# Depthwise convolutions of a focal-modulation block: diagonal products and vector taps replaced by products with banded matrices

## The reference, cut to what matters

```python
y = einsum('bhwc,cd->bhwd', layernorm(x), Wf) + bf
q, ctx, gates = y[..., :32], y[..., 32:64], y[..., 64:68]
ctx_all = 0
for l, k in enumerate((k0, k1, k2)):          # depthwise, 3x3, 5x5, 7x7, 'SAME'
    ctx = gelu(dwconv_same(ctx, k))
    ctx_all = ctx_all + ctx * gates[..., l:l + 1]
ctx_global = gelu(mean(ctx, axis=(1, 2)))
ctx_all = ctx_all + ctx_global * gates[..., 3:]
x_out = q * (einsum('bhwc,cd->bhwd', ctx_all, Wh) + bh)
x = x + (einsum('bhwc,cd->bhwd', layernorm(x_out) * gamma + beta, Wp) + bp)
# then a recurrent layer, a two-directional state-space layer, a mixture of experts
```

## Time and profile before

| | |
|---|---|
| median of 3 runs | 858.18 us (853.11, 858.18, 858.95) |
| the profiled execution | 853.12 us, span 851.2 us |
| PE | 680.4 us busy, 80% of the span, 8288 MATMUL |
| PEld | 416.7 us busy, 49% |
| DVE | 701.4 us busy, 82% |
| ACT | 362.5 us busy, 43% |
| POOL | 478.3 us busy, 56% |
| mean granted clock of TensorE | 0.943 |

### The profile page before, as it was taken

One profiled execution on the slowest core, in us unless ns is written; L12 is line 12 of the kernel. 1 busy time (PEld: TensorE's weight loads), 2 busy tenths in 40 slices (PEclk: granted clock), 3 DMA queues, 4 the chain that ended last, 5 costly groups with the idle time before them and its releaser, 6 DMA issues. The chain is left out here.

```text
span 851.2 us, 19699 instructions
## 1 busy us (share of the span) xinstructions
PE 680.4 (80%) x8288; PEld 416.7 (49%) x8288; DVE 701.4 (82%) x917; ACT 362.5 (43%) x577; POOL 478.3 (56%) x243
## 2 busy tenths in 40 slices
PE   7887786779977658887888788888878887787496
PEld 3554453346645325555555555555554554454142
DVE  3998889664334089999999999999999999995785
ACT  2230001146642755655565555555655665431000
POOL 5000000000001089999999999999999999990000
PEclk9999998789979959999999999999999999998697
DMA  4000000000000737887778777877897787740001
GB/s 177 5 4 4 4 5 4 2 1 1 1 2 16 181 100 187 204 225 205 198 207 229 196 208 202 224 207 201 204 225 202 201 227 206 197 113 2 1 12 47
DMA packets 35080, 102.95 MB, mean 121 GB/s; under 512 B 6768, under 2 KB 8944, under 8 KB 34992
## 3 DMA queue, kind: packets, MB, share of 16 engines
q1 hardware_dynamic: 34768, 100.84, 45.3%
q0 software_dynamic: 224, 0.85, 0.2%
HBM read 98.13 MB, written 3.54 MB: 119 GB/s over the span
## 5 line engine op out<-in xcount | busy, mean ns | idle before, releaser
L547 POOL TENSOR_TENSOR ring<-ring,big 128x1152 f32<-128x1152 f32 x74 | 193.7, 2630 | 4.0 <-DVE ring L923 4.0
L189 PE MATMUL banks<-ring,main_params 128*128 128x288 f32 x592 | 174.0, 423 | 0.6 <-POOL ring L547 0.6
L701 ACT ACTIVATE big<-big,small 128x576 f32<-128x576 f32 x192 | 142.5, 765 | 30.3 <-DVE ring L923 15.8
L923 DVE TENSOR_TENSOR_SCAN ring<-big,banks 128x576 f32<-128x576 f32 x111 | 146.1, 1339 | 1.5
L911 DVE TENSOR_TENSOR banks<-banks,big 128x576 f32<-128x576 f32 x192 | 141.3, 743 | 2.9 <-POOL big L533 1.6
L523 POOL COPY big<-normed 128x288 f32<-128x288 f32 x8 | 3.0, 430 | 242.2 <-DVE normed L443 242.2
L1234 PE MATMUL banks<-big,selectors 96*128 96x512 bf16 x192 | 72.8, 390 | 70.2 <-DVE ring L923 39.9
L189 PEld LDWEIGHTS banks<-ring,main_params 128*128 128x128 f32 x592 | 105.3, 191 | 36.1 <-issue 4.0
L377 PE MATMUL banks<-big 32*32 32x288 f32 x3712 | 96.7, 429 | 21.5 <-issue 17.5
L547 POOL TENSOR_TENSOR normed<-normed,big 128x1152 f32<-128x1152 f32 x36 | 94.4, 2631 | 0.9 <-DVE normed L923 0.9
L781 DVE SCALAR_TENSOR_TENSOR big<-big 128x288 f32<-128x288 f32 x216 | 93.6, 510 | 0.0
(11 more groups left out here) (179 smaller groups left out, 1016.3 us busy)
## 6 DMA issues: line engine op xcount, KB each, us to landing
big<-bc_rows SPq DMA_DIRECT2D x256, 288.0 KB, 4.3
big<-bc_rows SPq DMA_DIRECT2D x128, 144.0 KB, 4.4
bc_rows<-big SPq DMA_DIRECT2D x16, 144.0 KB, 3.3
residual<-x_in SPq DMA_DIRECT2D x2, 576.0 KB, 6.0
out<-big SPq DMA_DIRECT2D x16, 72.0 KB, 1.8
experts<-experts_in SPq DMA_DIRECT2D x1, 896.0 KB, 9.4
main_params<-main_in SPq DMA_DIRECT2D x1, 639.0 KB, 8.2
big<-front_in POOLq DMA_DIRECT2D x1, 574.5 KB, 5.9
```

The source lines that it names most:

```text
L189: last = nc.tensor.matmul(PS[rows, 2 * p + a, 0:HALF], lhsT, rhs[:, bass.ds(at + a * HALF, HALF)], start=start, stop=stop, skip_group_chec ...
L547: nc.gpsimd.tensor_tensor(slots, slots, CT[k % 5], ALU.mult).then_inc(weighted, 1)
L701: nc.scalar.activation(out, DT[b % 3], ACT.Exp, scale=ANEG[:, s:s + 1]).then_inc(decay_set, 1)
L923: nc.vector.tensor_tensor_scan(slot, DECAY[m % 3], place, 0.0, ALU.mult, ALU.add).then_inc(scanned, 1)
```

## The change

The first layer is laid out anew. The context goes through the convolutions with image columns on the partitions: partition 32 j + x holds column x of the images j of all four groups, and the free axis is channel, group, row (`CT0`, `A1`, `B2`, `C3`). A convolution of one channel along a row is then a product with a 32 x 32 banded matrix, and the rows' offsets dy are taken by shifted reads. For every level, every block k of four channels, every offset dy, every strip r and every channel q of the block there is one 32 x 32 matmul with 4 (24 - |dy|) columns, at most 96. No tap is left on VectorE.

The new pieces: the banded matrices are computed on the host and loaded (11,520 columns of fp32 on 128 partitions, 5.9 MB, three transfers on SP between x and the rest of `main_params`). ctx and the gates are produced row by row, with the image row as the stationary operand and 36 columns of Wf as the moving one. VectorE copies them out in three instructions, multiplies every level with its gate (`gate`), and turns the products back to channels on partitions (`turn`, 32 x 32 transposes). Sums for the global context are 48 matmuls with 64 columns.

```diff
-            for cp in CP:
-                nc.gpsimd.memset(cp, 0.0).then_inc(pads_zero, 1)
...
+            for l in range(LEVELS):
+                part = slice(TW_AT[l], (TW_AT + [TW_W])[l + 1])
+                sp.dma_start(TW[:, part], toeplitz_in[:, part]).then_inc(toeplitz_loaded[l], 16)
...
+            def ctx_rows(ys):
+                for y in ys:
+                    a, at = y // (H // 2), y % (H // 2) * (C + 4)
+                    for g in range(GROUPS):
+                        rows = slice(C * g, C * (g + 1))
+                        for j in range(J):
+                            last = nc.tensor.matmul(PS[C * j:C * (j + 1), 4 * a + g, at:at + C + 4],
+                                                    XNW[rows, j * L + y * W:j * L + y * W + 32], fpar("wcg")[rows, :],
+                                                    start=True, stop=True)
...
+            def conv_block(l, kh, k):
+                src = by_channel((CT0[:, 0:TB], A1, B2)[l])
+                for i, dy in enumerate(offsets(l)):
+                    ys = slice(max(0, -dy), H - max(0, dy))
+                    there = slice(ys.start + dy, ys.stop + dy)
+                    for r in range(GROUPS):
+                        rows = slice(C * r, C * (r + 1))
+                        for q in range(GROUPS):
...
+                            last = nc.tensor.matmul(dst.rearrange("p (g y) -> p g y", g=GROUPS)[:, :, ys], TW[rows, at:at + 32],
+                                                    src[rows, k, q, :, there], start=i == 0, stop=i == KS[l] - 1)
...
+            for l in range(LEVELS):
+                pe.wait_ge(toeplitz_loaded[l], 16)
+                for kh in range(2):
+                    if l == 0:
+                        pe.wait_ge(ctx_dve, 2 + kh)
...
+                        pe.wait_ge(gelu_set, 2 * (l - 1) + kh + 1)
...
+                    for k in range(4 * kh, 4 * kh + 4):
+                        last = conv_block(l, kh, k)
...
+                    last.then_inc(tap_mm, 1)
+            for kh in range(2):
+                pe.wait_ge(gelu_set, 2 * 2 + kh + 1)
...
+                for y in range(H):
+                    last = nc.tensor.matmul(PS[:, 4 * kh, 0:64], fpar("sumx"), per_row[:, :, y], start=y == 0, stop=y == H - 1)
+                last.then_inc(sum_mm, 1)
...
+            for a in range(2):
+                dve.wait_ge(mod_mm, a + 1)
+                for j in range(J):
...
+                    nc.vector.scalar_tensor_tensor(out=GLOBAL[:, here], in0=GLOBAL[:, here], scalar=GADD[:, j:j + 1],
+                                                   in1=PS[:, 4 * a + j, 0:HALF], op0=ALU.mult, op1=ALU.add).then_inc(glob_added, 1)
```

More of the change, by code:

```diff
@@ L248, in build_program @@
[L248 to L259, removed]
@@ L507, in _ @@
             pool.dma_start(RSEL, rows_in).then_inc(rows_loaded, 16)
-            for cp in CP:
-                nc.gpsimd.memset(cp, 0.0).then_inc(pads_zero, 1)
[L511 to L517, removed]
+            nc.gpsimd.memset(XNW[:, N:N + 8], 0.0).then_inc(tail_zero, 1)
             for a in range(2):
@@ L593, in _ @@
+            act.wait_ge(gadd_mm, 1)
+            nc.scalar.activation(GADD, PS[:, 5, 0:J], ACT.Copy).then_inc(gadd_set, 1)
             ln_act(act, 1, 1)
@@ L1054, in _ @@
             pe.wait_ge(front_loaded, 16)
-            pe.wait_ge(main_loaded, 16)
-            for a in range(2):
-                pe.wait_ge(ln_out, a + 1)
-                strips(quad_bank(a), own(fpar("wctx")), plain(XN, a), True, True).then_inc(ctx_mm, 1)
+            pe.wait_ge(tail_zero, 1)
+            def ctx_rows(ys):
[7 more added lines that the diff above has]
+                                                    start=True, stop=True)
+                return last
@@ new lines, in _, with spread_gates @@
+            pe.wait_ge(ln_out, 1)
+            ctx_rows(range(H // 2 - 1))
+            pe.wait_ge(ln_out, 2)
+            ctx_rows([H // 2 - 1]).then_inc(ctx_mm, 1)
+            ctx_rows(range(H // 2, H)).then_inc(ctx_mm, 1)
+            def spread_gates():
+                gates = CT0[:, TB:TB + 4 * ROWS].rearrange("p (l c) -> p l c", l=4)[:, 0:3:2, :]
+                pe.wait_ge(ctx_dve, 3)
+                for j in range(J):
+                    rows = slice(C * j, C * (j + 1))
+                    last = nc.tensor.matmul(PS[:, 4 + j, 0:2 * ROWS], fpar("rep")[rows, :], gates[rows], start=True, stop=True)
+                last.then_inc(rep_mm, 1)
@@ L1107, in _ @@
-            pe.wait_ge(gelu_set, 4 + 2 * GROUPS)
-            pe.wait_ge(gated, 6 * GROUPS)
-            for a in range(2):
-                strips(quad_bank(a), own(fpar("wh")), plain(ALLT, a), True, False)
-            for j in range(J):
-                pe.wait_ge(glob_added, j + 1)
-                for a in range(2):
-                    last = nc.tensor.matmul(PS[:, 4 * a + j, 0:HALF], fpar("wh"),
-                                            ALLC[:, j * L + a * HALF:j * L + (a + 1) * HALF], start=False, stop=True)
@@ new lines, in modulate @@
+            def modulate(a):
+                pe.wait_ge(turned_p, 2 * 1 + a + 1)
+                strips(quad_bank(a), own(fpar("wh")), lambda rows, c: turned_row(P1T, a)[rows, c, :, 0:W], True, False)
+                by_j(a, P0T, False)
+            pe.wait_ge(glob_set, 1)
+            modulate(0)
+            pe.wait_ge(turned_p, 2 * 2 + 1)
+            by_j(0, P2T, True).then_inc(mod_mm, 1)
+            pe.wait_ge(glob_mask, 1)
+            for g in range(GROUPS):
+                last = nc.tensor.matmul(PS[C * g:C * (g + 1), 5, 0:J], fpar("whu"), GMASK[:, g * J:(g + 1) * J],
+                                        start=True, stop=True)
```

335 lines of the change are left out of this document (165 added, 170 removed).

## The result

The changed kernel took 893.5 us (median of 4 runs, 891.9 to 900.2), the kernel before beside it 855.6 us (4 runs, 848.6 to 859.0). The ratio is 1.047, with a 95% interval from 1.038 to 1.056. It is slower, as forecast, and the time lies within the range of 852 to 897 us, but the loss is 38 us where 22 were worked out. The profiled execution took 892.8 us, with a span of 890.9 us where before it was 851.2. XO was complete at 197.5 us instead of 156.4: 41.1 us later. The untouched rest took 693.4 us instead of 694.7. The whole loss lies ahead of XO.

The account below looks back on a forecast made before the run. TensorE was taken as bound by loading its instructions, 256 at a time; 11.5 us for the stretch plus 10.5 for the tail gave 22.0 on 853.1, 875.1, stated as 877 us after a run-spread allowance; range 852 to 897.

Parts of the forecast that it names:

- What bounds the kernel: First layer up to the tail: TensorE waits for instruction loading, some 3.8 us per piece of 256 instructions, whatever it holds.
- The count: Context, convolutions and linear parts: 2324 calls, 9296 instructions, 36.3 pieces; last convolution ends at 154.6 us, 11.5 later.
- VectorE's copy of ctx: Before level 0 of the convolutions: a new wait of about 1.5 us, hidden while the next piece loads.
- One piece is free as before: Start of the stretch at 19.6 us: first instructions lie ready, so 35.3 of 36.3 pieces cost loading time.
- The transfers: Loading 5.9 MB of matrices: no waits for them; sharing engines with first instruction packets may cost a microsecond or two.
- The tail: From last convolution to XO complete: 23.8 us instead of 13.3, 10.5 more, bounds 7.4 and 21.5.
- The sums: In the tail, two sums of 48 LDWEIGHTS and MATMUL pairs each: 13 us, mostly full clock; bounds 11.5 and 24.
- the rival of the slow clock: Sparse work leaves TensorE at half clock when the tail's sums start; they take 24 us, total 888 us; chance 0.12.
- The modulating products: In the tail, TensorE's modulation of 96 calls lies beside VectorE's last `turn` of 3.2 us, adding nothing.
- The array-bound case: Stretch up to the tail: fewer columns shorten pieces to about 1.1 us, total 786 us; chance 0.10.
- The fetch starts sooner: Stretch up to the tail: narrow products bring packets earlier, about 3.1 us a piece, total 850 to 853 us; chance 0.14.
- the signs named beforehand: First layer: 36 to 39 instruction packets, starts 3.7 to 3.9 us apart, over 2 us "issue" each, VectorE mostly idle.

Follow-up runs that it names:

- narrow: Changed kernel with all convolution row offsets but the middle computed for one of four image groups only, calls unchanged: 892.8 us.
- before_narrow: Kernel before the change, every TensorE tap product but the first of a half cut from 288 to 96 columns, calls kept: 852.4 us.
- half_instr: `dve_sums` with the convolutions' products in bf16, one LDWEIGHTS and one MATMUL a call instead of two each: 818.6 us, 0.956 of the kernel before.
- fewer: Changed kernel with three of the 7x7 level's seven row offsets, 512 calls or 2048 instructions less: 862.7 us.
- late: Changed kernel with the matrices of levels 1 and 2 (4.3 MB), and loads queued behind them, requested only once the context is half made: 896.0 us.
- dve_sums: Changed kernel with the global context's sums over rows taken by VectorE reductions, leaving TensorE one 64-column product for each half: 882.4 us.
- side_taps: Kernel before the change, 26 of its 166 taps moved from TensorE and VectorE to ScalarE (multiplying) and GpSimd (adding): 890.2 us, ratio 1.042.

## Why the prediction was right, and where it was not

**What bounds the kernel: right.** The reading of the earlier trace rows holds in every run. Columns taken away left the starts 3.45 and 3.73 us apart and moved the end by 2 to 3 us (`narrow`, `before_narrow`); instructions taken away moved it by 3.6 and 3.9 us for each 256 (`half_instr`, `fewer`). The rule "mostly hidden" of the Trainium skill, page "Runtime: NRT & Kernel Launch", section "Instruction fetch mechanics", doesn't hold here: 36.6 us of the convolutions were this wait, up to 2.3 us at a crossing.

**The count: right.** From the second piece (26.00 us) to the last convolution (162.1) the windows have 640 + 1534 + 2351 = 4525 MATMUL, 35.35 pieces, in 136.1 us: 3.85 us a piece, where 35.3 x 3.8 stood in the sum. That is 2.0 us more, within its bounds. 1.4 of it is the piece at 44.13 us, which took 5.20: VectorE's copy of ctx was booked as hidden, since its wait "falls within a piece whose instructions run in less than 3.04 us", and it was not, as that piece was not waiting for instructions. Nobody waited for the matrices, which had landed by 23 us; the prediction, by the rate of a single load, had the last part at 65. Apart from that one wait, VectorE was off the path until the tail.

**The start of the stretch: the step that failed there.** By the sum the second piece should have started at about 19.6 + 0.9 = 20.5 us, and it started at 26.00. Three things make up the 5.5 us.
- The stretch began at 20.3 instead of 19.6: 0.7 us.
- "One piece is free as before": it was not. With no load in the way (`late`) the second piece still starts 3.42 us after the first, an ordinary distance, where 0.9 stood: 2.5 us. The first piece was there, the packet of the second moved only once the stretch had begun.
- The transfers: 5.74 us instead of 3.42, so 2.3 us. "They share the engines with the first instruction packets, which may cost a microsecond or two": the prediction had named this, nearly at its size, and booked it at nothing in the sum. `late` shows the cause by moving it.

Together: 154.6 + 0.7 + 2.5 + 2.3 + 2.0 = 162.1 us, the measured end.

**The tail: the larger miss.** 23.8 us were worked out, and 35.4 measured (162.1 to 197.5).
- The sums: 20.7 us instead of 13. This is the rival of the slow clock, which gave them 24: 0.50 was granted, and a pair took 0.213 us. The 0.25 read from the earlier trace rows was too high, as its 0.50 us for two loads includes the whole passage of the second. The 0.12 for the full clock was about right (some 0.11 in `dve_sums`); the clock assumed was not. The forecast rested on the 0.99 of the earlier trace rows, which was the clock of an array busy 99.8 of 123.5 us. The changed stretch made it busy for less than half of 26:44, and there the clock was at 0.50. The prediction gave this rival a chance of 0.12, from a clock that had only been read under the other load. `dve_sums` takes the sums away, and XO comes 15.8 us sooner after the last Gelu.
- The modulating products: 2.67 and 1.76 us, where the prediction said that they lay "beside" the last `turn`. The first takes 4.91 us against 2.90 of the transpose, and the second 4.19 us; VectorE waited for both, 4.4 us that were booked at nothing.
- The last transpose took 2.90 us (3.2 in the sum), the XO instructions without the wait 6.5 us (6.5), and from the sums to the transpose it was 0.9 (1.1).

7.7 + 4.4 - 0.3 - 0.2 = 11.6 us, the miss of the tail. (The bound of 7.4 us for it should be 7.9 by the prediction's own terms; nothing rests on it.) With the 7.5 of the stretch it would be 19.1 more; against that stand 1.3 us in the rest behind XO. 22.0 + 19.1 - 1.3 = 39.8, the difference of the spans (39.7). The median came out at +37.9.

**The rivals.** The array-bound case would have given 786 us and fell. "The fetch starts sooner" fell nearly: some starts are 3.45 us apart with light pieces, so single pieces gained up to 0.3 us of 3.73, not 0.6, and the mean of 3.85 gained nothing. The slow clock came true in mechanism, and its 888 us are nearer to the 893.5 than the forecast's 877; the rest is the start of the stretch and the modulating products.

**How much of the hit was owed to the range.** The measured 893.5 us lie outside the forecast's own 869 to 892. They lie within 852 to 897 because the range was made to hold the slow clock too. Of the signs named beforehand, the 36 instruction packets in the first layer came as said (17 to 162 us), and so did a VectorE that is mostly idle. The idle time at the pieces of the convolutions was 1.5 us on average and not over 2, since their records at the lower clock last up to 2.4 us.

## What to carry to other kernels

When TensorE runs hundreds of small products in a row, count its instructions before its columns: here 256 of them cost 3.5 to 4.0 us, however little work they hold, and the sign is idle time put to "issue" every 128 MATMUL beside one packet on the instruction queue. A reform that keeps the number of instructions is worth nothing there, and one that halves it (here bf16, one LDWEIGHTS and MATMUL for a product instead of two) took 32 to 37 us off the kernel before, in either layout, at the price of precision and together with the other changes named above. When such a stretch gets sparse, ask what the tail costs at the lower clock (here 20.7 us for sums booked at 13), and do not expect a gain from moving large loads within it: two places were tried, and the stall came along.

## What the runs showed of the hardware that I had not expected

- Loads hold up the loading of instructions: with the DMA engines 90% busy TensorE stood 4.5 us ahead of the second piece, and 2.2 without loads; with the loads moved, two pieces took 5.92 us each instead of some 3.5.
- TensorE stayed at 1.2 GHz (0.50) for 21 and for 29 us in which it was busy nearly all the time, with 128 x 128 fp32 weights and 64 columns, and also with bf16 products of 512 columns between them. Two such loads took 0.50 us at that level and 0.30 at a granted clock of 1.00 (`dve_sums`).
- VectorE and GpSimd hold each other up whole: in `side_taps` a VectorE instruction of 0.51 us took 2.9 beside GpSimd's adds of 2.66, and an add stood for 22.65 us until VectorE's run of taps was over.
- A part of the program that nobody touched (everything behind XO) took 693.4 to 701.4 us over the profiled kernels.
